# Row 0 of a fused attention and mixture kernel: another order for scores, turns and products with V, a later shortcut sum, and norms moved in three queues

## What is computed

```
y   = layernorm(x)                                   # plain
x1  = y + proj(window_attention(layernorm(y)*g1+b1)) # 16 heads of 16, each token sees 15 keys
a   = x1 + fc2(gelu(fc1(layernorm(x1)*g2+b2)))       # hidden 1024, exact gelu
x   = x + a
z   = layernorm(x)
out = x + al*main(z) + (1-al)*sum of 2 experts of 8 chosen by mean(z)   # each 256->1024->256, tanh gelu
```

## Time and profile before

| what | value |
|---|---|
| median of three runs | 1947.49 us |
| the profiled execution's own time | 1946.44 us |
| its span, first to last instruction | 1944.70 us |
| PE busy | 1916.3 us (99%), 23,696 matmuls |
| DVE, ACT, POOL busy | 1392.7, 1191.7, 855.9 us (72, 61, 44%) |
| PE's share of the chain that ended last | 96% |
| mean granted TensorE clock | 0.998 |

### The profile page before, as it was taken

One profiled execution on the slowest core, in us unless ns is written; L12 is line 12 of the kernel. 1 busy time (PEld: TensorE's weight loads), 2 busy tenths in 40 slices (PEclk: granted clock), 3 DMA queues, 4 the chain that ended last, 5 costly groups with the idle time before them and its releaser, 6 DMA issues.

```text
span 1944.7 us, 57593 instructions
## 1 busy us (share of the span) xinstructions
PE 1916.3 (99%) x23696; PEld 1727.3 (89%) x23696; DVE 1392.7 (72%) x2331; ACT 1191.7 (61%) x1867; POOL 855.9 (44%) x784
## 2 busy tenths in 40 slices
PE   7899999999999999999999999999999999999999
PEld 6789889898998989899888998989999898998998
DVE  7576776867767687777867768687686877768744
ACT  5575665756657566575755657566575665757554
POOL 3537254362534626245271543625346252452725
PEclk9999999999999999999999999999999999999999
DMA  3121210312112121121311203121021311212111
GB/s 113 55 75 55 68 52 23 91 50 82 49 30 82 42 85 48 42 77 32 86 56 54 65 23 91 50 76 55 26 83 45 85 46 41 78 34 86 45 61 55
DMA packets 147342, 116.25 MB, mean 60 GB/s; under 512 B 17836, under 2 KB 139912, under 8 KB 147080
## 3 DMA queue, kind: packets, MB, share of 16 engines
q1 hardware_dynamic: 146504, 111.78, 19.7%
q10 hardware_dynamic: 576, 0.79, 0.1%
HBM read 85.52 MB, written 8.39 MB: 48 GB/s over the span
## 4 chain that ended last, share of the span: by engine, by line
PE 96%; DVE 2%; ACT 1%; issue 1%; POOL 0%; SPq 0%; DMA 0%; ACTq 0%; POOLq 0%; DVEq 0%
PE psB L236 56%; PE psA L236 27%; PE psA L1137 4%; PE psA L1100 3%; PE psA L1112 3%; PE psA L1013 2%; PE psA L1154 0%; DVE hr_lo L544 0%; DVE zT_lo L568 0%; ACT qm L883 0%; DVE pr L625 0%; DVE pr L634 0%; ACT hr_hi L854 0%; DMA pT<-in_L_attn_norm_b 0%; DVE smax L623 0%
## 5 line engine op out<-in xcount | busy, mean ns | idle before, releaser
L544 DVE TENSOR_TENSOR hr_lo<-hf,hr_hi 128x512 fp32r<-128x512 f32 x512 | 476.6, 931 | 457.0 <-ACT hr_hi L854 456.5
L444 POOL TENSOR_SCALAR wx_hi<-raw 128x512 fp32r<-128x512 f32 x256 | 201.6, 787 | 715.6 <-DMA raw<-in_L_ffn_W2e 379.2
L854 ACT ACTIVATE hr_hi<-hf 128x512 fp32r<-128x512 f32 x512 | 324.1, 633 | 277.3 <-PE psB L236 189.2
L446 POOL TENSOR_TENSOR wx_lo<-raw,wx_hi 128x512 fp32r<-128x512 f32 x256 | 398.4, 1556 | 21.4
L236 PE MATMUL psB<-wx_hi,hr_hi 128*128 128x256 f32 x1024 | 287.5, 281 | 0.7 <-DVE hr_lo L544 0.6
L236 PE MATMUL psB<-wx_hi,hr_lo 128*128 128x256 f32 x1024 | 286.4, 280 | 0.0
L236 PE MATMUL psB<-wx_lo,hr_hi 128*128 128x256 f32 x1024 | 285.7, 279 | 0.0
L850 ACT ACTIVATE hf<-psB,b1x 128x512 f32<-128x512 f32 x256 | 175.3, 685 | 167.3 <-PE psB L236 166.2
L236 PE MATMUL psB<-z_hi,wx_hi 128*128 128x512 f32 x512 | 211.9, 414 | 0.0
L236 PE MATMUL psB<-z_hi,wx_lo 128*128 128x512 f32 x512 | 202.7, 396 | 0.4 <-issue 0.4
L236 PEld LDWEIGHTS psB<-wx_hi,hr_hi 128*128 128x128 f32 x1024 | 192.5, 188 | 10.5 <-DVE hr_lo L544 1.3
(11 more groups left out here) (159 smaller groups left out, 4777.5 us busy)
## 6 DMA issues: line engine op xcount, KB each, us to landing
raw<-in_L_ffn_W1e SPq DMA_DIRECT2D x256, 128.0 KB, 2.2
raw<-in_L_ffn_W2e SPq DMA_DIRECT2D x256, 128.0 KB, 2.2
vb<-vs SPq DMA_DIRECT2D x64, 144.0 KB
out_x<-acc SPq DMA_DIRECT2D x32, 256.0 KB, 2.2
vb<-vs SPq DMA_DIRECT2D x64, 120.0 KB
xin<-in_L_attn_x SPq DMA_DIRECT2D x15, 512.0 KB, 3.7
tm<-in_L_ffn_b2e SPq DMA_DIRECT2D x32, 128.0 KB, 3.0
raw<-in_L_attn_fc_w SPq DMA_DIRECT2D x8, 256.0 KB, 4.5
```

Of the source, the lines that this page charges most:

```text
L444: g.tensor_scalar(wx[0][:, s, :], raw[:, s, :], 1.0, 0.0, ALU.mult, ALU.add).then_inc(w_hi.sem, 1)
L446: g.tensor_tensor(wx[1][:, s, :], raw[:, s, :], wx[0][:, s, :].bitcast(f32), ALU.subtract).then_inc(w_lo.sem, 1)
L544: v.tensor_tensor(hr[1][:, c % 2, :], hf[:, c % 3, :], hr[0][:, c % 2, :].bitcast(f32), ALU.subtract).then_inc(h_lo.sem, 1)
L854: a.activation(hr[0][:, c % 2, :], hf[:, c % 3, :], ACT.Copy).then_inc(h_hi.sem, 1)
```

## The change

It touches the order of programs; no operand or size changes. On PE: the transpose of `small` moves behind the transposes of the first norm; in row 0, `turn(0, 1)` runs ahead of `attend(0, 0)`, which moves behind `scores(0, 3)`; `turn(0, 3)` runs ahead of `attend(0, 2)`; the transposes of row 1's norm move ahead of `chunk_down` of m6; `scores(1, 0)` moves from behind the third norm's transposes to behind `chunk_up` of f0; the warm matmuls are dealt out anew (7 + 72 for 6 + 73). On POOL the shortcut of row 0 waits for the low part of m1. On DVE the copy to `smallT` moves behind the first three weight subtractions, and `shifts(0)` behind `values(0, 0)`. On ACT the `table` call ahead of the first norm goes, and `z3` of row 0 moves ahead of `query_blocks(1, 1)`. Rows 1 to 15 keep their order, but for `scores(1, 0)`.

```diff
--- before.py
+++ after.py
@@ -450,6 +450,8 @@
                 g.tensor_tensor(y[:, :, :], y[:, :, :], bproj[:, :].unsqueeze(1).to_broadcast([P, NT, D]), ALU.add).then_inc(yb.sem, 1)
 
             def shortcut(t):
+                if t == 0:
+                    g.wait_ge(h_lo.sem, mc(0, 1) + 1)
                 g.wait_ge(x1.sem, x1.all(t))
                 g.wait_ge(t2_lo.sem, t2_lo.all(t))
                 if t > 0:
@@ -515,9 +517,10 @@
                 if i % 2 == 0:
                     v.wait_ge(rstd_first.sem, rstd_first.at(0, i * HALF // NT))
                 v.tensor_scalar(tn[:, i, :], xin[:, i, :], mv[:, 0, i, 0:1], rs[:, NT + i:NT + i + 1], ALU.subtract, ALU.mult).then_inc(z1_s.sem, 1)
-            v.wait_ge(small_ps.sem, 1)
-            v.tensor_copy(smallT[:, :], psA[:, 3, 0:NSM]).then_inc(small_t.sem, 1)
             for n in range(FIRST):
+                if n == FIRST - 1:
+                    v.wait_ge(small_ps.sem, 1)
+                    v.tensor_copy(smallT[:, :], psA[:, 3, 0:NSM]).then_inc(small_t.sem, 1)
                 dst = pieces[n][1]
                 v.wait_ge(p_hi.sem, split_value(n))
                 v.tensor_tensor(dst[1], raw_piece(n), dst[0].bitcast(f32), ALU.subtract).then_inc(p_lo.sem, 1)
@@ -720,7 +723,6 @@
                 v.tensor_tensor(acc[:, :, :], acc[:, :, :], b2sum.unsqueeze(1).to_broadcast([P, NT, D]), ALU.add).then_inc(acc_b.sem, 1)
 
             gained_T(0, tr1, t1_f1, t1_hi, t1_lo, 1, oG1, oB1)
-            shifts(0)
             v.wait_ge(consts.sem, N_CONST)
             v.wait_ge(small_t.sem, 1)
             for c in range(KD):
@@ -728,6 +730,7 @@
             query_blocks(0, 0)
             v.wait_ge(rows_in.sem, rows_in.all(0))
             values(0, 0)
+            shifts(0)
 
             def alphas():
                 v.tensor_scalar(al[:, 1:2], al[:, 0:1], 0.1, 1.0, ALU.max, ALU.min).then_inc(alpha_s.sem, 1)
@@ -922,7 +925,6 @@
                     rows = slice(GW * gr, GW * gr + GW)
                     a.activation(zT[0][rows, c, LEFT:LEFT + T], psA[rows, 2 + gr, :], ACT.Copy).then_inc(tA_hi.sem, 1)
 
-            table(ACT.Gelu_apprx_tanh)
             gained_T(0, tr1, t1_f0, t1_f1, t1_hi, 0, oG1, oB1)
             keys(0, 0)
             a.wait_ge(hbias_s.sem, KD)
@@ -993,7 +995,8 @@
                     elif q == SPLIT + 11 and t + 1 < ROWS:
                         if t == 0:
                             query_blocks_first(t + 1, 0)
-                        query_blocks(t + 1, 1)
+                        else:
+                            query_blocks(t + 1, 1)
                     elif q == NQ:
                         if t:
                             a.wait_ge(up.sem, fc(t, NCH - 1) + 1)
@@ -1001,13 +1004,11 @@
                         for c in range(KD):
                             a.wait_ge(tr3.sem, tr3.at(t, c))
                             a.activation(z3[0][:, c, :], psA[:, 2 + c, :], ACT.Identity, accum_out=msum[:, c:c + 1]).then_inc(z3_hi.sem, 1)
+                        if t == 0:
+                            query_blocks(t + 1, 1)
 
         @block.tensor
         def _(pe):
-            pe.wait_ge(small_in.sem, small_in.all(0))
-            pe.wait_ge(consts.sem, 4)
-            pe.transpose(psA[:, 3, 0:NSM], small[:, :], ident[0:NSM, 0:NSM]).then_inc(small_ps.sem, 1)
-
             def transposes(tr, c, src, bank):
                 for i in range(NT):
                     last = pe.transpose(psA[:, bank, i * P:(i + 1) * P], src[:, i, c * P:(c + 1) * P], ident[:, :])
@@ -1154,19 +1155,28 @@
                     last = pe.matmul(psA[:, 1, 0:E] if t else psB[:, 2, 0:E], msum[:, k:k + 1].to_broadcast([P, P]), wg[:, k, :], start=k == 0, stop=k == KD - 1)
                 last.then_inc(router.sem, 1)
 
+            def next_norm(row):
+                pe.wait_ge(z1_s.sem, z1_s.all(row))
+                for c in range(KD):
+                    pe.wait_ge(gelu.sem, mc(row - 1, KH - 2 + c) + 1)
+                    transposes(tr1, c, tn, c)
+
             def warm(n):
 
                 for _ in range(n):
                     pe.matmul(psB[:, 0, :], wqkv[0][:, 0, 0:P], wqkv[0][:, 0, 0:T], start=True, stop=True)
 
 
-            WARM = {3: 18, 4: 4, 7: 4, 8: 12, 10: 3, 11: 4, 12: 8, 14: 12, 16: 8}
-
+            WARM = {3: 20, 4: 4, 8: 10, 10: 3, 12: 9, 14: 17, 16: 9}
+
+            pe.wait_ge(consts.sem, 4)
             pe.wait_ge(z1_s.sem, z1_s.all(0))
             for c in range(KD):
                 transposes(tr1, c, tn, c)
+            pe.wait_ge(small_in.sem, small_in.all(0))
+            pe.transpose(psA[:, 3, 0:NSM], small[:, :], ident[0:NSM, 0:NSM]).then_inc(small_ps.sem, 1)
             pe.wait_ge(p_hi.sem, split_value(1))
-            warm(6)
+            warm(7)
             pe.wait_ge(p_lo.sem, split_value(3))
             pe.wait_ge(small_t.sem, 1)
             pe.wait_ge(t1_lo.sem, t1_lo.all(0))
@@ -1180,13 +1190,14 @@
                 for q in range(NQ + 2):
                     if q < NQ and there(ORDER[q][0], t):
                         chunk_up(t, *ORDER[q])
+                    if q == SPLIT + 8 and t == 0:
+                        next_norm(t + 1)
                     if q >= 2 and there(ORDER[q - 2][0], t):
                         chunk_down(t, *ORDER[q - 2])
                     if t == ROWS:
                         continue
                     if q == 0:
-                        if t != 1:
-                            scores(t, 0)
+                        scores(t, 0)
                         if t:
                             pe.wait_ge(z3_lo.sem, z3_lo.at(t - 1, 0))
                         values(t, 1)
@@ -1206,17 +1217,23 @@
                     elif q == 5:
                         scores(t, 2)
                     elif q == 6:
-                        attend(t, 0)
+                        if t:
+                            attend(t, 0)
                         turn(t, 1)
                     elif q == 7:
                         scores(t, 3)
+                        if t == 0:
+                            attend(t, 0)
                     elif q == 8:
                         attend(t, 1)
                     elif q == 10:
                         turn(t, 2)
                     elif q == 11:
+                        if t == 0:
+                            turn(t, 3)
                         attend(t, 2)
-                        turn(t, 3)
+                        if t:
+                            turn(t, 3)
                     elif q == 12:
                         attend(t, 3)
                         if t == 0:
@@ -1230,11 +1247,8 @@
                             transposes(tr2, c, tm, c)
                         if t == 0:
                             pe.wait_ge(p_lo.sem, split_value(12))
-                    elif q == SPLIT + 8 and t + 1 < ROWS:
-                        pe.wait_ge(z1_s.sem, z1_s.all(t + 1))
-                        for c in range(KD):
-                            pe.wait_ge(gelu.sem, mc(t, KH - 2 + c) + 1)
-                            transposes(tr1, c, tn, c)
+                    elif q == SPLIT + 8 and 0 < t and t + 1 < ROWS:
+                        next_norm(t + 1)
                     elif q == SPLIT + 10 and t + 1 < ROWS:
                         pe.wait_ge(t1_lo.sem, t1_lo.all(t + 1))
                         project_qk(t + 1, 0, 1, 0)
@@ -1248,13 +1262,11 @@
                             pe.wait_ge(x2.sem, x2.at(t, c))
                             transposes(tr3, c, tm, 2 + c)
                     elif q == NQ + 1:
-                        if t == 0:
-                            scores(t + 1, 0)
-                        elif t + 1 < ROWS:
+                        if 0 < t and t + 1 < ROWS:
                             pe.wait_ge(kT_s.sem, kT_s.at(t + 1, 0))
                             values(t + 1, 0)
                             pe.wait_ge(qm_odd.sem, qm_odd.at(t + 1, 3))
-                        else:
+                        elif t:
                             pe.wait_ge(gelu.sem, mc(t, KH - 1) + 1)
                         route(t)
                     if t == 0 and q in WARM:
```

## The result

The changed kernel is slower: median 1952.56 us (1949.58 to 1955.57, 7 runs) against 1946.65 us (1945.29 to 1947.56, 7 runs), ratio 1.0032 with a 95% interval of 1.002 to 1.0044. The profiled execution took 1952.31 us with a span of 1950.5, 5.8 us more than before. Forecast were 1944.4 us and a range that ended at 1947.2.

What follows compares the result with a forecast made beforehand. PE, busy almost without gaps behind 110 us, was taken as the bound, so only an earlier `scores(1, 1)` counts. Terms -2.7 (prologue inside) + 1.7 - 1.05 = -2.05 gave 1944.4 us from 1946.44, range 1938.3 to 1947.2.

Steps and rivals of the forecast that it cites:

- Where the time comes from: Whole kernel: the effect arises ahead of 110 us, through the start of `scores(1, 1)`, and is carried to the end one for one.
- Prologue: Up to the first projection: transposes moved ahead and gains starting earlier on ACT bring it to 12.75 us, -0.7 us.
- Attention to `scores(0, 3)`: Row 0: turn 1 needs just the masks, so `scores(0, 3)` start at 33.9 instead of 38.99 us.
- Code and clock: Row 0 to `project`: 3.4 us per 127-matmul block, then half-clock warms; `project` at 54.8 us, -2.7 with the prologue inside.
- Rival C: Row 0: clock falling at about 38.5 us stays at half past `project`; +7.6 on the forecast, 1952.0 us; chance 0.05.
- third stop: Row 0: another stop of 2 us within `attend(0, 2)` and `(0, 3)`, which take 4.6 us together.
- fc1/fc2 of row 0: Shortcut's wait saves 1.3 us at first, but delays POOL's splits, SP's loads and ACT's pieces 17 to 20: +1.7 us.
- Into row 1: Projection of row 1 to `scores(1, 1)`: z3 first and scores behind f0 remove waits, 13.1 instead of 14.15 us, -1.05.
- A: Row 0's attention: code does not hold PE up, the old stop was a DMA crowd; -7.65, 1938.8 us; chance 0.25.
- B: fc1/fc2 of row 0: ACT's loads are no obstacle, -1.2 instead of +1.7; -4.95 in all, 1941.5 us; chance 0.16.

Runs made afterwards that it cites:

- e10: Kernel before plus 640 tiny matmuls at q = 3 of row 0, going round four quarters of the array: 1958.66 us (1 run).
- e2: Changed kernel without the wait of row 0's shortcut for the low part of m1: 1950.74 us, ratio 1.0022.
- e3: Changed kernel with the old order into row 1 (scores(1, 0) ahead of the router, last query block ahead of z3): 1953.6 us, ratio 1.0036.
- e4: Changed kernel without the ten warm matmuls at q = 8 of row 0: 1954.23 us, ratio 1.0037.
- e5: Changed kernel with half of row 0's product with V left out (64 matmuls instead of 128 per attend): 1941.08 us, ratio 0.9972.
- e6: Changed kernel with half of row 0's product with V left out and the old attention order: 1945.25 us, ratio 0.9997.
- e1: Changed kernel with row 0's attention and the loop's warm matmuls as before the change: 1948.02 us, ratio 1.0004.
- e12: Changed kernel with old attention order, no shortcut wait, and five more warm matmuls at q = 31 and 32: 1947.04 us, ratio 1.0004.
- e8: Changed kernel with the old order of row 0's attention and without the shortcut's wait: 1943.44 us, ratio 0.9988.
- e9: Changed kernel without shortcut wait, row 0's attend(0, 1) behind turn(0, 2), five warm matmuls instead of ten ahead of that: 1948.98 us, ratio 1.0016.
- e13: As e12, but with 13 instead of 18 warm matmuls at q = 3: 1944.25 us, ratio 0.9993.
- e11: Changed kernel with old attention order, no shortcut wait, and the old order into row 1 as well: 1945.26 us, ratio 0.9996.
- e14: Kernel before with five more warm matmuls at q = 14 of row 0: 1947.13 us, ratio 1.0006.
- e7: Kernel before plus 640 tiny matmuls at q = 3 of row 0, all writing the same 32 rows: 1974.87 us (1 run).

## Why the prediction was wrong

**Where the time comes from** was right: ahead of `scores(1, 1)` all but 0.4 us of the 5.8.

**Prologue**: -0.7 forecast, -0.8 measured; ACT started the gains at 9.71 us without a table load, and the load ahead of the first exp went too. The drain that the Trainium skill counts on top of a table load (ScalarE: Activation LUTs, What ACT_TABLE_LOAD costs) did not show as time given back.

**Attention to `scores(0, 3)`**: 33.9 us forecast, 33.90 measured, and unit 2 was normalised at 40.6 (40.3 forecast).

**Code and clock is the step that failed.** The prediction had 54.8 us for `project`; it came at 59.83. The mechanism was right and its term mis-sized, -2.7 against +2.3.

Three amounts make up the 5.0 us. First, the stops in `attend(0, 0)` and `(0, 1)` ended at 38.89 and 42.34 instead of 38.1 and 41.4. The 3.45 us between them are the forecast's price; the 0.8 were lost ahead of them, where the packets of q8 start 3.5 and 3.8 us apart. 3.4 us per block is the floor (e10: 3.5 and 4.3), and I used it as the price; with this `attend(0, 2)` started at 49.04, 1.0 late.

Second, `attend(0, 2)` and `(0, 3)` took 7.1 us instead of 4.6, since there was a stop in `attend(0, 2)` too. By my count its block had had 9 us to come, yet no packet of q8 starts between 40.0 and 49.28 us in the trace. It is no accident of this execution: the same gap is 10.9 us in e2, 9.2 in e3 and 8.7 in e4, where the ten warm matmuls are left out. Why this packet comes so late is open, and with it part of the largest of the three amounts.

Third, the copies and warm matmuls to `project` took 3.7 us instead of 2.2, at half clock: the clock came back at 46 as forecast and fell again at 52.6, 1.0 us after the end of the stop of 1.7 us.

Rival C had the half clock up to `project`, but as one long spell, so that its 1952.0 us next to the measured 1952.56 are in part luck; and 0.05 was far too little for it: each of the two spells followed on stops, and the prediction itself had a third stop.

The 5.0 us are those of one execution; e2 and e3, with the same program up to `project`, have it at 62.34 and 60.75 us. A slip of no weight: by the prediction's own count the boundary in `attend(0, 2)` before the change lies 89 or 90 matmuls in, not 85; its time of 51.3 us stays.

e5, e6 and e10 together show that code is the cause, e4 that the ten warm matmuls, which I counted at what they last, cost nothing: PE was held up all the same.

The Trainium skill's rule that fetching is hidden behind the issue floor (Runtime: NRT & Kernel Launch, Instruction fetch mechanics) does not hold for these bursts; by it e10's 640 matmuls would have run in one piece.

**fc1/fc2 of row 0**: +1.7 forecast, +2.2 measured (2.2 against e2). SP's loads began 12.2 us behind fc1, 12.3 in the forecast (82.47 - 70.31 against 80.4 - 68.09); ACT stood 5.48 us ahead of piece 17, PE 1.86 ahead of m6 (2.5 forecast). `h_low` of m0 took 0.69 us, and the 1.17 us are gone, as forecast. The +2.2 came near the +1.7 by two errors that offset each other: without the half clock near 87 us the section is +1.2 to +1.4 (e3, e5, e6: 27.5 to 27.6 us, against 26.2 before), less than forecast, and the clock, which the prediction did not have here, adds 0.9.

**Into row 1**: -1.05 forecast, +0.95 measured. At full clock it would have been -0.6 (e1 and e12: 13.55 and 13.6 us, against 14.15), so that the forecast gain was too large even without the clock. `f0` began 7.9 us behind the projection, as forecast, but the clock fell at 107.2 us, and the scores took 1.8 instead of 1.15 us. The prediction had no clock in this section, though PE waits twice there, 0.7 and 0.9 us. It fell in this section in the profiles of the changed kernel, e2, e5 and e8, and not in those of e1, e4, e6 and e9, which have the same order there, nor with warm matmuls in the gaps (e12, e13). In the old order (the kernel before, e3, e11, e14) it never fell. What decides among equal orders is open.

**Rivals**: A (code does not hold PE up) was refuted by the four stops and by e10; B (ACT's loads no obstacle) by ACT's own wait.

## What to carry to other kernels

Reordering a dense part of PE's program moves not only data dependencies but also where its code is fetched: count instructions between the waits, and where several hundred small matmuls stand back to back, at less than some 3.5 us for each 128, put slow work (matmuls of 512 columns, chunks) between them or halve the instructions before gaining time on the chain. When a wait is put ahead of an operation that other engines' programs are queued behind (POOL's splits, SP's loads, ACT's copies), follow it to the last of them. And price the clock behind each stop by itself, the short ones too: one spell of 3.4 us took 0.9 us in fc1/fc2 of row 0 and 1.3 to 1.6 in the step into row 1, more than the whole saving that was forecast there.

## What the runs showed of the hardware

- PE's code comes in blocks of about 127 matmuls here (weight load and matmul each; 23,696 matmuls in 187 packets, 510 in four blocks), and no two packets of the instruction queue q8 start less than 3.2 us apart in any of the 16 profiles. In the burst groups of 128 began 4.3 and 3.5 us apart. Blocks can come much later than that: in the changed kernel 9.3 us lie between two packets, and PE then stood 1.68 us for the second, for no reason that was found.
- Tiny matmuls into the same rows start every 0.031 us, those going round four quarters every 0.01 us.
- PE can be busy without a gap and have the clock at half: 22 us in e7 (36 to 58 us).
- Seven executions of the changed kernel lie 6.0 us apart, seven of the kernel before 2.3. Whether its stops are the cause was not tried. In e8, a faster execution goes with a higher clock: the four fastest of 11 (1941.7 to 1943.0 us) have a mean granted clock of 0.999 to 1.000, the five slowest (1944.6 to 1946.7 us) 0.996 or 0.997.
